# Flamingo gated attention block on one Trainium2 core: the value product in fp16 parts, and the order of scores, value product and copies

## The reference, cut to what matters

```python
x   = x + tanh(g_xattn[0]) * xattn(layernorm(x), ctx, ctx, Wq, Wk, Wv, Wo, bo, mask)
x   = x + tanh(g_ffn[0])   * ffn(layernorm(x), w_gate, w_up, w_down)
# xattn: x is (64, 128, 256), 16 heads of 64, INNER = 1024
qh, kh, vh = split_heads(q @ Wq), split_heads(k @ Wk), split_heads(v @ Wv)
dots = einsum('bhid,bhjd->bhij', qh, kh) * 64**-0.5
dots = where(mask[:, None, None, :] | causal, -max, dots)
out  = einsum('bhij,bhjd->bhid', softmax(dots), vh)
return out @ Wo + bo
```

## Time and profile before

| what | value |
|---|---|
| median of 3 runs | 1624.48 us (1622.92 to 1630.77) |
| the profiled execution | 1626.47 us |
| its span, first to last instruction | 1624.6 us |
| PE busy | 94% of the span |
| DVE / ACT / POOL busy | 85% / 77% / 64% |
| granted TensorE clock, mean | 0.982 |

### The profile page before, as it was taken

The page is one execution under the profiler, slowest core; times in us unless marked ns, Lnnn a source line. Parts: engine busy times, 40 slices in busy tenths (PEclk is TensorE's granted clock), DMA queues, the critical chain, the costliest instruction groups (busy, mean ns, idle before and its releaser), DMA issues. The chain is left out here.

```text
span 1624.6 us, 38058 instructions
## 1 busy us (share of the span) xinstructions
PE 1530.6 (94%) x12556; PEld 1251.8 (77%) x12556; DVE 1385.1 (85%) x2247; ACT 1253.4 (77%) x3222; POOL 1033.8 (64%) x1004
## 2 busy tenths in 40 slices
PE   7899999999999999999999999789989997995998
PEld 5787887877877878878778788677767776775887
DVE  7888888888888888888888889878887998998996
ACT  5887887888778778878887787566758998885674
POOL 3988988888888889888888888600006664740000
PEclk9999999999999999999999999999998999997999
DMA  6554445444444544454444445369957884755664
GB/s 195 118 127 103 105 106 122 104 92 115 106 105 103 126 102 105 107 121 104 92 115 106 105 103 98 86 205 344 321 215 262 282 287 153 276 227 187 218 214 145
DMA packets 347365, 252.23 MB, mean 155 GB/s; under 512 B 287792, under 2 KB 317616, under 8 KB 344368
## 3 DMA queue, kind: packets, MB, share of 16 engines
q1 hardware_dynamic: 347312, 251.58, 55.1%
HBM read 105.25 MB, written 76.02 MB: 112 GB/s over the span
## 5 line engine op out<-in xcount | busy, mean ns | idle before, releaser
L496 ACT ACTIVATE prob<-masked,neg_max 128x128 f32<-128x128 f32 x1024 | 397.6, 391 | 35.1 <-DVE neg_max L662 31.6
L431 POOL TENSOR_TENSOR prob_parts<-prob,prob_parts 128x512 f16<-128x512 f32 x254 | 310.3, 1241 | 2.7 <-ACT prob_parts L504 1.6
L426 POOL TENSOR_TENSOR prob<-prob,scaled 128x512 f32<-128x512 f32 x256 | 271.6, 1061 | 20.1
L660 DVE TENSOR_TENSOR masked<-score,mask_add 128x512 f32<-128x512 f32 x256 | 174.6, 682 | 74.0 <-PE score L963 67.9
L504 ACT ACTIVATE prob_parts<-prob 128x512 f16<-128x512 f32 x254 | 159.0, 627 | 75.6 <-POOL prob L426 71.7
L496 ACT ACTIVATION_READ_ACCUMULATOR prob<-masked,neg_max 128x1 f32 x1024 | 193.3, 189 | 0.0
L662 DVE TENSOR_REDUCE neg_max<-masked 128x4 f32<-128x512 f32 x256 | 175.6, 686 | 8.8
L438 POOL TENSOR_TENSOR probT<-turn 128x512 f32<-128x512 f16 x125 | 173.2, 1386 | 0.0
L1723 POOL TENSOR_SCALAR xThi<-n_x 128x1024 fp32r<-128x1024 int16 x15 | 43.8, 2919 | 202.9 <-DMA n_x<-n_x_d 166.8
L976 PE MATMUL y<-wo_hi,o_hi 128*128 128x256 f32 x508 | 148.3, 292 | 15.9 <-DVE o_lo L667 15.2
L424 POOL TENSOR_TENSOR scaled<-rsums,pscale 128x4 f32<-128x4 f32 x256 | 66.4, 259 | 124.0 <-DVE rsums L654 123.9
(11 more groups left out here) (249 smaller groups left out, 4485.5 us busy)
## 6 DMA issues: line engine op xcount, KB each, us to landing
gate<-gate_d SPq DMA_DIRECT2D x30, 768.0 KB, 4.3
n_x<-n_x_d SPq DMA_DIRECT2D x25, 512.0 KB, 4.9
gate_d<-stage SPq DMA_DIRECT2D x8, 1536.0 KB, 5.5
n_u_d<-w_raw SPq DMA_DIRECT2D x16, 768.0 KB, 4.1
stage<-n_u_d SPq DMA_DIRECT2D x16, 768.0 KB, 6.0
gate_d<-gate SPq DMA_DIRECT2D x7, 1536.0 KB, 5.5
x_in<-in_x SPq DMA_DIRECT2D x16, 512.0 KB, 3.9
ctx_in<-in_ctx_columns SPq DMA_DIRECT2D x16, 512.0 KB, 4.8
```

Of the source, the lines that this page charges most:

```text
L426: gp.tensor_tensor(prob[:, h], prob[:, h], scaled[:, h, :].rearrange("p (b o) -> p b o", o=1).broadcast_to([P, NB, P]), ALU.mult).then_inc ...
L431: gp.tensor_tensor(prob_parts[:, h, 1], prob[:, h].rearrange("p b k -> p (b k)"), prob_parts[:, h, 0], ALU.subtract).then_inc(prob_low, 1)
L496: nc.scalar.activation(prob[:, h, b, :], masked[:, h, b, :], ACT.Exp, bias=neg_max[:, h, b:b + 1], accum_out=psums[:, h, b:b + 1]).then_in ...
L660: nc.vector.tensor_tensor(masked[:, h], score[h][:], mask_add[:], ALU.add).then_inc(masked_done, 1)
```

## The change

- `times_v` no longer uses fp32. The values are kept as two fp16 parts, high and low (`v16`), and the turned fp16 halves of the probabilities (`turn`) are used as they are: high by high, high by low, low by high. 24 fp16 matmuls of 128 columns take the place of 8 fp32 ones. `probT`, `join_prob` and `join_second` are gone, and `turn_prob` and PE wait for `pv_done` and `prob_turned` directly.
- To fit fp16, values are scaled by a bound, made once a group: `ctx_top` (a DVE maximum over `ctx_in`), `value_bound` (four tiny fp32 matmuls on PE), `value_scale` and `output_unit` (three tiny DVE operations). `residual` multiplies by `y_unit`.
- All eight value copies of a group are now an ACT copy of the high part (`values_high`) and a DVE low part (`values`).
- PE: the first value projection of a step goes ahead of the output product, and the scores ahead of `times_v`.
- ACT: `high_prob` of head 1 goes from the end of a step to behind the next step's `qT` copy.
- DVE and POOL: `normalise` is split over c = 5 and c = 6, `second_max` and `residual` go to the end of their steps, the bias addition goes from c = 6 to c = 1 of the next group.

```diff
-        v_sb = sb("v_sb", [P, NB, INNER])
+        v16 = sb("v16", [P, NB, 2, 2, VH], F16)
@@ POOL step @@
-                if old:
-                    join_second(u - 3, (c + 1) % 2, NC // 2 * g + (c - 1) // 2)
-                if c == 6 and new:
-                    gp.wait_ge(xres_loaded, 16 * (g + 1))
...
+                if c == 1 and not (isinstance(g, int) and g == 0):
+                    add_bias(g - 1)
@@ ACT @@
+            def values_high(g, i, n):
+                b, before = nth(g, i)
+                if n == 0:
+                    act.wait_ge(v_scaled, 4 * g + 3)
+                act.wait_ge(projected[b], before + 1)
+                nc.scalar.activation(v16[:, n % NB, n // NB, 0], proj[b][:], ACT.Copy, scale=v_mul[:, 0:1]).then_inc(v_high, 1)
@@ ACT step @@
+                if not isinstance(g, int) or 2 <= u < U + 2:
+                    high_prob(u - 2, 1, (c + 1) % 2, NC // 2 * g + (c - 1) // 2)
...
-                if soft:
-                    high_prob(u - 1, 1, c % 2, NC // 2 * g + c // 2)
@@ DVE @@
+            def values(g, jobs):
+                for i, n in jobs:
+                    b, before = nth(g, i)
+                    dve.wait_ge(v_high, NC * g + n + 1)
+                    nc.vector.scalar_tensor_tensor(v16[:, n % NB, n // NB, 1], proj[b][:], v_mul[:, 0:1], v16[:, n % NB, n // NB, 0],
+                                                   ALU.mult, ALU.subtract).then_inc(copied[b], 1)
+            def ctx_top(g):
+                dve.wait_ge(ctx_loaded, 16 * (g + 1))
+                nc.vector.tensor_reduce(c_top[:], ctx_in[:], X, ALU.max, apply_absolute_value=True).then_inc(v_scaled, 1)
@@ DVE, before the first step @@
+            nc.vector.tensor_reduce(w_top[:, 0], staged(2), X, ALU.max, apply_absolute_value=True)
+            dve.wait_ge(w_loaded[5], 16)
+            nc.vector.tensor_reduce(w_top[:, 1], staged(5), X, ALU.max, apply_absolute_value=True)
+            ctx_top(0)
             w_low_part(3)
@@ PE, times_v @@
                 for b in range(NB):
-                    for h in range(2):
-                        last = nc.tensor.matmul(pv[h * HD:(h + 1) * HD, b, :], v_sb[:, b, c * P + h * HD:c * P + (h + 1) * HD],
-                                                probT[:, h, b, :], start=True, stop=True)
+                    for n, (m, t) in enumerate(((0, 0), (0, 1), (1, 0))):
+                        for h in range(2):
+                            at = c % NB * P + h * HD
+                            last = nc.tensor.matmul(pv[h * HD:(h + 1) * HD, b, :], v16[:, b, c // NB, m, at:at + HD],
+                                                    turn[:, slot, h, t * NB + b, :], start=(n == 0), stop=(n == 2))
@@ PE step @@
+                if first:
+                    scores_free(g, c, u)
+                    scores(g, c, u)
+                    value_bound(0)
                 if nxt:
                     transpose_in(g, *ts[0])
+                if new:
+                    for i, n in jobs_of(c, "v")[:1]:
+                        value(g, i, n)
                 if oldest:
                     out_product(u - 4, (c - 4) % NC)
                 if nxt:
                     transpose_in(g, *ts[1])
+                    value_bound(g + 1)
                 if new:
-                    for i, n in jobs_of(c, "v"):
+                    for i, n in jobs_of(c, "v")[1:]:
                         value(g, i, n)
+                if new and not first:
+                    scores_free(g, c, u)
+                    pe.nop(nofuse=True)
+                    scores(g, c, u)
                 if old:
-                    times_v(u - 3, co, (g, c, u) if new else None)
-                if new:
-                    if not old:
-                        scores_free(g, c, u)
-                    scores(g, c, u)
+                    times_v(u - 3, co, (c + 1) % 2, NC // 2 * g + (c - 1) // 2)
```

More of the change, by code:

```diff
@@ L41 @@
 PSCALE = 32768.0
+VMAX = 60000.0
+VTINY = 1e-30
 def split(hi, lo):
@@ L202, in attention @@
         xres_loaded = sem("xres_loaded")
-        probT_copied = [sem(f"probT_copied{h}") for h in range(2)]
+        v_high = sem("v_high")
+        v_scaled = sem("v_scaled")
+        v_bound = sem("v_bound")
+        last_turned = sem("last_turned")
         pv_done = sem("pv_done")
@@ L357, in turn_prob @@
                 sp.wait_ge(prob_low, 2 * u + h + 1)
-                wait(sp, probT_copied[h], u - 1)
+                wait(sp, pv_done, u - 1)
                 sp.dma_start_transpose(out=turn[:, u % 2, h], in_=prob_parts[:, h].rearrange("p e n -> p (e n)")).then_inc(prob_turned[h][u % 2], 16)
@@ L522, in step @@
                     nc.scalar.activation(qT[:], proj[b][:], ACT.Copy, scale=SCALE).then_inc(copied[b], 1)
+                if not isinstance(g, int) or 2 <= u < U + 2:
+                    high_prob(u - 2, 1, (c + 1) % 2, NC // 2 * g + (c - 1) // 2)
+                early = isinstance(g, int) and g == 0 and c < 3
+                vs = jobs_of(c, "v") if new else []
+                if early and c == 0:
+                    w_high_part(3)
+                if early:
+                    copy_k(g, c, u)
+                if early and c == 0:
+                    act.wait_ge(small_loaded, 32)
+                    nc.scalar.activation(tg[:], tg[:], ACT.Tanh).then_inc(gate_ready, 1)
+                if early and c == 2:
+                    w_high_part(6)
                 if soft:
                     exps(u - 1, 0)
-                if new:
+                if new and not early:
                     copy_k(g, c, u)
+                for i, n in vs[:1]:
+                    values_high(g, i, n)
                 if nxt:
@@ L532, in step @@
                     exps(u - 1, 1)
-                if isinstance(g, int) and g == 0 and c < 3:
+                if early and c < 2:
                     w_high_part(4 + c)
-                if new and c > 2:
-                    for i, n in jobs_of(c, "v"):
-                        b, before = nth(g, i)
-                        act.wait_ge(projected[b], before + 1)
-                        nc.scalar.activation(v_sb[:, n % NB, VH:2 * VH], proj[b][:], ACT.Copy).then_inc(copied[b], 1)
+                for i, n in vs[1:]:
+                    values_high(g, i, n)
                 if soft:
@@ L573, in _ @@
             attended(U - 2)
-            act.wait_ge(last_step, 1)
             act.wait_ge(pv_done, U - 1)
-            nc.scalar.activation(probT[:, 0], trans[:], ACT.Copy).then_inc(probT_copied[0], 1)
-            for n in range(4):
+            for h in range(2):
+                act.wait_ge(last_step, h + 1)
+                nc.scalar.activation(turn[:, 1, h, 0:NB], trans[:], ACT.Copy).then_inc(v_high, 1)
+                if h == 0:
+                    ffn_high_part(0)
+            for n in range(1, 4):
                 ffn_high_part(n)
@@ L614, in layernorm_moments, with normalise @@
                 moments(stats, mean, vare, stats_done, MOMENTS * g + NB, var_ready)
-            def normalise(g):
+            def normalise(g, first, end):
                 dve.wait_ge(rstd_ready, g + 1)
-                for b in range(NB):
+                for b in range(first, end):
                     last = nc.vector.tensor_scalar(x_in[:, b, :], x_in[:, b, :], mean[:, b:b + 1], rstd[:, b:b + 1],
                                                    ALU.subtract, ALU.mult)
-                last.then_inc(xn_ready, 1)
+                if end == NB:
+                    last.then_inc(xn_ready, 1)
             def low(g, i, n, high_before):
@@ L731, in step @@
                     second_norm(g - 1, NB // 2, NB)
-                if c == 6 and more:
-                    normalise(g + 1)
+                if c == 5 and more:
+                    normalise(g + 1, 0, NB // 2)
+                if c == 6 and after_first and more:
+                    second_max(g - 1)
+                if c == 3 and after_first:
+                    residual(g)
                 if isinstance(g, int):
```

125 lines of the change are left out of this document (67 added, 58 removed).

## The result

The changed kernel takes 1617.04 us, the median of 7 runs (1614.96 to 1618.04). The kernel before takes 1624.86 beside it (7 runs, 1622.92 to 1630.77). The ratio is 0.994, 95% interval 0.9926 to 0.9954 (the quotient of the means; that of the medians is 0.995). That is a gain of 7.8 us by the medians, inside the predicted range and under a third of the 26.5 us that were forecast.

The account below looks back on a forecast made before the run. PE was taken as the bound in the attention part. Product -24, waits -16.5, `value_bound` +7.5, no-operation +2.5 and start +4 sum to -26.5 us against the profiled 1626.47; counted from the median 1624.48, 1598, range 1584 to 1622.

Parts of the forecast that it names:

- The value product: PE's `times_v`: 0.83 us a step, 0.19 less than now; over 128 steps -24 us.
- Rivals B and C: Value product: B, fp16 no shorter than fp32, 1622 (0.10); C, weight loads in the open, 1.46 us, 1679 (0.06).
- The waits: PE's waits at c = 0, 5 and 7: of 2.0 us a group 1.1 gone; 15 groups, -16 us.
- The piece at c = 5: PE's extra time in step c = 5, expected to go along with the 0.8 us at c = 0.
- rival A: Waits only move: `kT` or first copies set PE's pace, ACT's longest queues at c = 0 and 7; 1614 (0.14).
- ACT: Four more value copies a group, 2.3 us, cost nothing; `kT` done at 5.0 us, needed at 5.7.
- Rival D: ACT becomes the bound, `kT` late by 0.3 us and more in each step; 1662 at half a microsecond (0.04).
- DVE: "Nothing": DVE's late work costs nothing up to 1.5 us into a step; the longest, c = 4's moments, runs 1.3.
- The no-operation: PE's no-operation and waits ahead of the scores: 0.02 us a step, +2.5 us.
- Start: Program start: three DVE reductions of 1.19 us ahead of the query weights' low part; +4 us, bounds 0 and +8.
- The likeliest case: The forecast itself: 1598 us, chance 0.66, its own range 1584 to 1610.
- The sign that was set for being wrong: Prediction is wrong if scores wait for `kT` in ordinary steps, or the group stays above 63 us.

Follow-up runs that it names:

- e_act_undone: Changed kernel with ACT's `high_prob` of head 1 back at the end of its step; 1618.88 us, ratio 0.9948 to the kernel before.
- e_scores_last: Changed kernel with the value product ahead of the scores again, value projection still first; 1616.44 us, ratio 0.993 to the kernel before.
- e_norm_early: Changed kernel with the first half of the next x's normalisation moved from c = 5's end to c = 3's start, `ctx_top` to c = 2; 1597.28 us.

## Why the prediction was right or wrong

**The value product: right in kind, a little better than taken.** Forecast 0.83 us, measured 0.80, against 1.02. Groups of weight loads, 300 to 900 us, answering to the earlier trace rows:

```profile
L999 PEld LDWEIGHTS pv<-turn,v 128*64 128x64 f16 x1824 | 53.1, 110 | 6.4
```

A load is recorded with 110 ns, yet 24 of them with their matmuls pass in 0.80 us. Eight fewer (four pairs, one for each half of the columns) take 0.22 us off, so a pair costs 0.055: the 128 columns streamed and nothing for the loads. The rule of the Trainium skill that I had weighed ("TensorE: Matmul & The Clock Gate", section "LDWEIGHTS (loading the stationary operand)") gives, as an estimate, 0.107 a pair if loads stand one after the other, 1.28 us for the product; the trace, with 0.80, disagrees. Rivals B and C are out by the same 0.80. The ordinary step came to 7.34 where I had 7.45. Of the 0.11, the product is 0.03 and the no-operation 0.02. The other 0.06 is between the pieces: the step less 5.55 of projections and output, the product and 0.83 of scores leaves 0.23 before and 0.16 now.

**The waits: right at c = 0 and c = 7, wrong at c = 5.** The 0.8 us at c = 0 went (9.90 to 8.75, of which 0.29 is every step's), and the 0.3 for `qT` at c = 7; the 0.2 for `kT` at c = 7 stayed, as forecast. The piece at c = 5, which was to go without being in the sum, did not, and `kT` is late in c = 5 and c = 6, behind late maxima and not, as rival A has it, behind long queues at c = 0 and c = 7. In ordinary steps PE has no wait, and `kT` is in time.

**ACT: right.** ACT's timeline in the ordinary step c = 2, which starts at 539.72, as the earlier trace rows:

```profile
541.50 0.60 ACT L530 ACTIVATE qT<-proj 128x512 f32<-128x512 f32 x1 [0.19 <-PE proj L932]
...
544.22 0.58 ACT L519 ACTIVATE kT<-proj 128x512 f32<-128x512 f32 x1
```

`kT` is done 5.08 us into the step where I had said 5.0. Rival D is out. ACT is busy 168.0 of 200 us in the middle of the loop, 84% where I had said some 86. But I priced ACT's added work for PE alone, and didn't ask what stands behind it in ACT's own queue.

**DVE: "Nothing". This is the step that failed.** It held that work running up to 1.5 us into a step costs nothing, and that the longest, the moments of c = 4, would run 1.3 us. The first half was about right (in c = 1 to 4 nothing is lost). The second was wrong, for three reasons. (1) Late work of c = 4 begins 7.06 us into the step, not 5.96, because `high_prob` of head 1 and a value copy (recorded with 0.67 us where it had 0.58) now stand ahead of the exps of head 1; e_act_undone shows 0.4 of this for `high_prob`, and the value copy's share (0.56 between starts) was not run by itself. (2) The step itself is 0.29 shorter, so its end comes earlier. (3) `normalise` was split, and I counted only that the x was ready in time, not where its first half lands: at the end of c = 5 behind `second_norm`, at up to 1.2 us an instruction. The moments ran 2.5 us into c = 5, which is the 1.1 of the earlier trace rows and 1.1 for (1) and 0.3 for (2), and the normalisation ran 3.1 us into c = 6. The check that was missing is small: the second reciprocal's place, plus the late work's length, minus the new step length, for every step with late work.

**value_bound:** forecast 0.5 a group, measured 0.88, so 0.11 an instruction, just above my upper bound of 0.8. **The no-operation:** 0.02 taken; e_scores_last, without it and with the old order, has the same ordinary step of 7.34. **Start:** forecast +4, measured +5.7 (second step's keys at 28.46, forecast 27; part of it is the clock). **End:** forecast 0, measured -0.9 behind the last group.

By steps, measured less forecast, per group: c = 0 -0.2, c = 1 to 4 -0.5, c = 5 +0.3, c = 6 +1.1, c = 7 +0.3, together +1.0. Fifteen groups are some 15 us; with 1.7 from the start and -0.9 at the end that is 16 of the 17 us by which the span's gain of 9.3 falls short of 26.5. The 19 us between 1598 and 1617 have 2 more, because the traced execution of the kernel before is 2.0 above its median. e_norm_early, which takes back the 1.2 of c = 6 and 0.2 of c = 7, comes to 1597.3. That it meets the forecast's number is in part luck: c = 0 to 4 are 0.7 a group better than forecast, c = 5 and c = 7 still 0.4 worse. What it shows is that the place of two DVE instructions (and of the maximum that made room) was worth the 20 us that had gone missing. The likeliest case was thus wrong as a case. No rival of mine named DVE as the one that becomes late; that the range held 1617 is luck, owed to rivals A and B, which did not happen.

Two numbers of the prediction do not follow from its own terms. A group of 63.8 less 1.5 for the product and 1.1 for the waits, with 0.5 for the bound and 0.2 for the no-operation, is 61.9, not 61.5; against 61.5 the miss of the group looks larger than it is. And 1598 less 16 is 1582, not 1584. The sign that was set for being wrong, a group above 63, did not show at 62.9 either: it was set too far out to catch this.

## What to carry to other kernels

When a bound engine's step gets shorter, ask for each other engine where in the step its last piece of work begins and where the step now ends; work "at the end" has no cover of its own. Compute it for the steps with the most extra work, not for the ordinary one. In a software pipeline with in-order queues, list what stands behind each waiting instruction on each engine: if the list comes back to the waiting instruction, the order can be worth more than any single duration (132 us here, some 20 of them the clock).

## What the runs showed of the hardware that I had not expected

A DVE operation on SBUF can last as long as the POOL operation beside it. In e_norm_early the moments of the first layer norm show both cases back to back on DVE:

```profile
534.13 1.03 DVE L622 TENSOR_SCALAR v_eps<-v_sum 128x4 f32<-128x4 f32 x1
535.20 0.16 DVE L624 SCALAR_TENSOR_TENSOR vare<-m_sq,v_eps 128x4 f32<-128x4 f32 x1
```

and POOL beside them:

```profile
534.10 1.04 POOL L431 TENSOR_TENSOR prob<-prob,scaled 128x512 f32<-128x512 f32 x1
536.37 0.20 POOL L429 TENSOR_TENSOR scaled<-rsums,pscale 128x4 f32<-128x4 f32 x1 [1.23 <-DVE rsums L667]
```

`v_eps` ends at 535.16, POOL's `prob` at 535.14; `vare`, with POOL idle, takes 0.16 where it took 1.08 beside `prob_parts` in the changed kernel. There, the eleven slow `vare` between 300 and 950 us all end within 60 ns of the end of a POOL operation, and `x_in` of 256 columns lasts between 0.38 and 1.26 us. This agrees with the Trainium skill, "SBUF — State Buffer", section "Who interferes with whom": a DVE operation with two SBUF inputs, or in a mode that uses both ports, and a GpSimd operation that reads SBUF exclude each other for a whole instruction, and the second to issue waits. So the price of moved DVE work depends on what POOL does at its new place. Here the two `x_in` at the end of c = 5 take 2.31 us beside POOL, and the two at the end of c = 6 take 0.71.

At the start, PE idle times of 1.42 and 1.08 us were followed by the 1.2 GHz level from 18 to 24 us. The kernel before has one wait of 2.60 us there, ahead of the matmul at 17.24, and keeps 1.00 from 10 to 40 us. In e_norm_early the same two waits last 0.87 and 0.53 us, and the granted clock is 1.00 there, but 0.75 from 10 to 14 us and 0.82 from 14 to 18. Which idle time is followed by such a dip, and where, stays open.
